# Delta rule: query norms as quadrant matmuls, alternating with the outputs' mean of squares in chunks of 256 columns

## What is computed

```python
q = heads(h @ Wq); k = heads(h @ Wk); v = heads(h @ Wv)
q = q / (norm(q) + 1e-6)
k = k / (norm(k) + 1e-6)
# for each token t, state s is 64x64 for each head and sequence
s = s * alpha[..., None]
pred = einsum('bhk,bhkv->bhv', k_t, s)
s = s + (beta * k_t)[..., None] * (v_t - pred)[:, :, None, :]
y_t = einsum('bhk,bhkv->bhv', q_t, s)
# then
y = y * rsqrt(mean(y * y, over a head) + EPS) * head_norm_w
```

## Time and profile before

| | |
|---|---|
| median of 3 runs | 2277.33 us (2270.29 to 2285.75) |
| the profiled execution | 2267.57 us, its span 2265.9 us |
| delta rule, 29 whole steps | 1063.5 to 1841.8 us of the span: 778.3 us, 26.8 us a step |
| busy over the span | PE 2017.6, PEld 1438.0, DVE 1503.7, ACT 1109.6, POOL 649.8 us |

### The profile page before, as it was taken

The page is one execution under the profiler, slowest core; times in us unless marked ns, Lnnn a source line. Parts: engine busy times, 40 slices in busy tenths (PEclk is TensorE's granted clock), DMA queues, the critical chain, the costliest instruction groups (busy, mean ns, idle before and its releaser), DMA issues. The chain is left out here.

```text
span 2265.9 us, 92374 instructions
## 1 busy us (share of the span) xinstructions
PE 2017.6 (89%) x41611; PEld 1438.0 (63%) x41611; DVE 1503.7 (66%) x3186; ACT 1109.6 (49%) x1913; POOL 649.8 (29%) x603
## 2 busy tenths in 40 slices
PE   4999997899877697979999999999999997988998
PEld 2666665566535484237888888888888873456446
DVE  7999984466567735766877777777787774344104
ACT  1344445366576765664555444454454543244334
POOL 5766661111130001213333333333333332001000
PEclk8999999899989999978999999999999998996998
DMA  3000000000000001000000000000000001002001
GB/s 95 3 3 3 3 3 2 6 3 3 2 4 11 1 2 32 0 0 4 5 4 4 4 4 4 4 4 4 4 5 4 4 5 52 0 1 75 0 0 38
DMA packets 34585, 23.28 MB, mean 10 GB/s; under 512 B 14857, under 2 KB 30161, under 8 KB 34194
## 3 DMA queue, kind: packets, MB, share of 16 engines
q1 hardware_dynamic: 34194, 17.38, 2.9%
HBM read 15.27 MB, written 2.10 MB: 8 GB/s over the span
## 5 line engine op out<-in xcount | busy, mean ns | idle before, releaser
L1747 PEld LDWEIGHTS psum<-dr_kq,dr_kSq 64*64 64x64 f32 x6144 | 199.4, 136 | 66.9 <-issue 56.9
L1747 PE MATMUL psum<-dr_kq,dr_kSq 64*64 64x64 f32 x6144 | 225.5, 222 | 8.2 <-DVE dr_G L2353 3.1
L2054 ACT ACTIVATE dr_Y<-psum 128x256 f32<-128x256 f32 x160 | 63.0, 394 | 313.1 <-PE psum L1753 312.1
L1747 PE MATMUL psum<-dr_GT,dr_Y 64*64 64x32 f32 x5120 | 186.7, 221 | 11.6 <-issue 11.0
L1753 PE MATMUL psum<-dr_G,dr_CT 64*64 64x32 f32 x5120 | 186.9, 223 | 0.2
L1747 PEld LDWEIGHTS psum<-dr_GT,dr_Y 64*64 64x64 f32 x5120 | 166.0, 135 | 15.7 <-issue 11.3
L1753 PEld LDWEIGHTS psum<-dr_G,dr_CT 64*64 64x64 f32 x5120 | 167.6, 136 | 0.8 <-issue 0.5
L2143 POOL TENSOR_TENSOR dr_kSq<-dr_kSq,dr_decay 128x256 f32<-128x256 f32 x128 | 99.0, 774 | 215.3 <-PE psum L1747 212.3
L2344 DVE COPY_PREDICATED dr_PT<-dr_level_masks,psum 128x256 f32<-128x256 uint32 x192 | 102.7, 535 | 83.0 <-PE psum L1747 80.4
L1753 PEld LDWEIGHTS psum<-dr_Y,dr_GT 64*64 64x64 f32 x4096 | 135.0, 136 | 33.7 <-issue 32.0
L1753 PE MATMUL psum<-dr_Y,dr_GT 64*64 64x32 f32 x4096 | 147.1, 220 | 7.1 <-issue 5.7
(11 more groups left out here) (385 smaller groups left out, 5541.8 us busy)
## 6 DMA issues: line engine op xcount, KB each, us to landing
topk_w<-in_L_ffn_w_dram SPq DMA_DIRECT2D x16, 256.0 KB, 5.9
attn_w_x_rows<-in_x_dram SPq DMA_DIRECT2D x4, 512.0 KB, 5.4
out_dram<-store_rows SPq DMA_DIRECT2D x4, 512.0 KB, 3.6
dout_w<-in_L_attn_Wff_dram SPq DMA_DIRECT2D x3, 256.0 KB, 3.0
attn_w_rows<-in_L_attn_Wq_dram SPq DMA_DIRECT2D x1, 256.0 KB, 5.4
attn_w_rows<-in_L_attn_Wk_dram SPq DMA_DIRECT2D x1, 256.0 KB, 4.8
attn_w_rows<-in_L_attn_Wv_dram SPq DMA_DIRECT2D x1, 256.0 KB, 4.2
attn_w_rows<-in_L_attn_Wo_dram SPq DMA_DIRECT2D x1, 256.0 KB, 3.8
```

The lines of the kernel that those rows point to most:

```text
L1747: last = nc.tensor.matmul(out(r), lhsT(r), rhs(r), start=True, stop=True)
L2054: act.activation(half_of(Y[l], l, 0), ZG[:, ZS].rearrange("p (m l) -> p m l", l=1 << l), ACT.Copy).then_inc(z_kept[l], 1)
```

## The change

The full-array matmul of the query norms leaves `norms`. The one of `head_norm` is split up. A new function `head_norms` stands where `head_norm` stood and issues both, in two chunks of 256 columns: for each chunk two `cross` matmuls of 64x64 for the queries into F1 and two `stay` matmuls of 64x64 for the outputs into E0. It waits for all that either needed.

As the query part crosses over, the squared queries must lie in the other half of the partitions. So `square` squares only the keys, and a new `square_queries` squares the queries in two instructions of 64 partitions each, reading one half and writing the other. In ACT's list `square_queries` follows `square_y`, `log_queries` moves behind `exp_norms`, and `query_eps` behind `inverse_y`. In `front` and `end`, which run once each, only one of the two sorts of matmul is issued.

```diff
@@ norms
             last.then_inc(n2_ready, 1)
-            nc.tensor.matmul(F1[:, :], w.head_sum[:, :], sq[:, 1, :], start=True, stop=True).then_inc(q2_ready, 1)
@@
-        def head_norm(w_, y):
-
-            u = par(w_)
+        def head_norms(w_, y):
+
             if y is not None:
                 pe.wait_ge(logn_ready, upto(y))
-            pe.wait_ge(floored, upto(w_))
-            nc.tensor.matmul(E0[:, :], w.head_mean[:, :], ysq[:, :], start=True, stop=True).then_inc(yms_ready, 1)
+                pe.wait_ge(q_squared, upto(y))
+            if w_ is not None:
+                pe.wait_ge(floored, upto(w_))
+            for at in (slice(0, 256), slice(256, 512)):
+                if y is not None:
+                    last_q = cross(lambda r: F1[r, at], lambda r: w.head_sum[r, r], lambda r: sq[r, 1, at])
+                if w_ is not None:
+                    last_m = stay(lambda r: E0[r, at], lambda r: w.head_mean[r, r], lambda r: ysq[r, at])
+            if y is not None:
+                last_q.then_inc(q2_ready, 1)
+            if w_ is not None:
+                last_m.then_inc(yms_ready, 1)
@@ PE, front
             values(y)
+            head_norms(None, y)
             diagonal(y)
@@ PE, end
-            head_norm(w_, None)
+            head_norms(w_, None)
@@ PE, half
-            if w_ is not None:
-                head_norm(w_, y)
+            if w_ is not None or y is not None:
+                head_norms(w_, y)
@@ ACT
-            act.activation(sq[:, :, :], kSq[par(y)][:, :, :], ACT.Square).then_inc(sq_ready, 1)
+            act.activation(sq[:, 0, :], kSq[par(y)][:, 0, :], ACT.Square).then_inc(sq_ready, 1)
+
+        def square_queries(y):
+
+            for j, r in enumerate(HALVES):
+                last = act.activation(sq[HALVES[1 - j], 1, :], kSq[par(y)][r, 1, :], ACT.Square)
+            last.then_inc(q_squared, 1)
@@ ACT, front
             square(y)
+            square_queries(y)
             exp_beta(y)
@@ ACT, half
                 square_y(w_)
             if y is not None:
+                square_queries(y)
                 log_norms(y)
-                log_queries(y)
                 exp_beta(y)
             keep_z(x, 3)
             if y is not None:
                 exp_norms(y)
-                query_eps(w_, y)
+                log_queries(y)
             if w_ is not None:
                 log_y(w_)
                 inverse_y(w_)
+            if y is not None:
+                query_eps(w_, y)
             keep_z(x, 4)
```

More of the change, by code:

```diff
@@ L1675, in delta_rule @@
     (zeroed, consts, h_staged, spikes_staged, logits, beta_ready, sig_ready, counted, pushed, raised, floored, paired, gates_ready, kq_logits, kSq_ready,
-     sq_ready, kq_ready, n2_ready, summed, counts_kept, biased, e_ready, logn_ready, norm_ready, length_ready, squared, denom_ready,
+     sq_ready, q_squared, kq_ready, n2_ready, summed, counts_kept, biased, e_ready, logn_ready, norm_ready, length_ready, squared, denom_ready,
      inverted, strong, turned, logq_ready, nq_ready, q2_ready, q_eps_ready, g0_made, gt0_made, v_ready, v_kept, diag_ready, diag_kept, rv_ready, rv_kept,
@@ L1680, in delta_rule @@
         "zeroed", "consts", "h_staged", "spikes_staged", "logits", "beta_ready", "sig_ready", "counted", "pushed", "raised", "floored", "paired", "gates_ready",
-        "kq_logits", "kSq_ready", "sq_ready", "kq_ready", "n2_ready", "summed", "counts_kept", "biased", "e_ready", "logn_ready",
+        "kq_logits", "kSq_ready", "sq_ready", "q_squared", "kq_ready", "n2_ready", "summed", "counts_kept", "biased", "e_ready", "logn_ready",
         "norm_ready", "length_ready", "squared", "denom_ready", "inverted", "strong", "turned", "logq_ready", "nq_ready", "q2_ready", "q_eps_ready", "g0_made",
```

## The result

| | before | after |
|---|---|---|
| median of 20 runs each | 2275.18 us (2262.32 to 2294.90) | 2263.89 us (2251.84 to 2276.59) |
| ratio | | 0.9954, 95% interval 0.9932 to 0.9976 |
| profiled execution, span | 2265.9 us | 2261.2 us |

The account below looks back on a forecast made before the run. PE was taken to set the pace, with DVE at 77% behind it. 33.6 us of PE work saved minus 1.9 us of waiting gave 31.7 us, from the median 2277.33 to 2245.6 us, 1.4% faster; range 2234 to 2271.

Parts of the forecast that it names:

- The array's work: PE in `norms` and `head_norms`: 1.06 us removed plus 0.06 us saved, 1.12 us a step, 33.6 us.
- Rivals B and C: `head_norms` quadrants: B two at a time, 2271 us, chance 0.09; C one at a time, 2322 us, chance 0.04.
- The rule of the Trainium skill on one PSUM bank and two row tiles: `head_norms`: different row tiles can't access one PSUM bank at once, so quadrants go two at a time; kept as a rival.
- DVE against POOL: `scale(x, 4)` on DVE loses 0.45 us behind POOL's `pair`; idle 0.46 us before `add_gt(x, 4)` covers it, costed at nothing.
- Rival A: After `pair`, POOL's `scale(x, 4)` goes first, DVE waits another 0.6 us, 18 us back, 2263.6 us; chance 0.16.
- `z_and_level(3)` waiting for `keep_ct(3)`: After `norms`, PE waits for DVE's `keep_ct(3)` in seven of 30 steps, about 1.9 us in all.
- The step that failed: PE sets the pace, its idle 1 to 2 us a step lying ahead of `norms`, waiting for ACT and DVE.
- The closing sentence: Wrong if PE's idle time ahead of `norms` grew by what it lost behind it; then DVE sets the step.

Follow-up runs that it names:

- the wide kernels: Kernels before and after the change with five parts each as one product of 512 columns, 280 records fewer a step; 0.9784 and 0.9705 of the kernel before.
- before_wide5: Kernel before the change with `level_zero`, `read_v`, `corrected`, `solve` and `outputs` each one product of 512 columns, 280 records fewer a step; ratio 0.9784.

## Why the prediction was wrong

**The array's work was right**, if by two errors that cancel. Forecast: `norms` 1.06 us shorter, the place of L1925 0.06. Measured: 0.94 and 0.19. `z_and_level(3)` starts 1.01 us after the first load of `norms` at the earliest and not 0.89. `head_norms` takes 0.70 us from its first weight load to the next part's in the step shown, not 1.00, but its last turn still runs then, and the first matmul of `g_and_gt(3)` starts 0.91 us after the first of `head_norms`. Sum 1.13 against 1.12. Rivals B and C are out: four turns, not eight or sixteen. The rule of the Trainium skill on one PSUM bank and two row tiles (TensorEngine Tiling (Array Packing), Restrictions and Gotchas) isn't borne out by the rows at 1201.02 to 1201.73 either, where each row group writes its own half of the bank's partitions.

**DVE against POOL was right in its cover.** The `scale` of decay on DVE went from 890 to 926 ns in the mean of 128, a seventh of a microsecond a step and not 0.45. The one of `scale(x, 4)` alone went from 0.96 to 1.13 us in the mean, where 1.45 was forecast. The wait of `add_gt` for PE fell from 14.6 us to 7.8, so the cover lasted. Rival A gave 2263.6 us, and 2263.9 was measured. That is chance: its mechanism, DVE giving the time back at `z_and_level(4)`, is not there. `diagonal, z_and_level(4)` takes 2.14 us in the mean, as before. A result that fits a rival's number isn't evidence for it.

**`z_and_level(3)` waiting for `keep_ct(3)` was right in kind**: by the times at which it ends, PE started late for it in 5 of 30 steps, 3.1 us in all where 1.9 was forecast. Of these, 2.1 us fall on the first step, where the kernel before lost 1.2 us in the same way. The view of waits, which covers the other 29, books 0.7.

**The step that failed** is the first one: that PE's idle time lies "ahead of `norms`, where PE waits for what ACT and DVE make", and that time taken from PE is taken from the path "as long as the other engines keep up". The other engines did keep up. PE's own instructions did not. The 1 to 2 us a step were mostly gaps on "issue" in the middle of parts, with no releaser, and I gave them to two engines that were already done. From that followed the missing term: 24 more records in a step and 1.1 us less to bring them in were costed at nothing. Measured, the time above the shortest parts rose by 0.77 us a step, 23 us:

- PE's gaps over 0.1 us: in the middle of a part 24.1 us in 41 gaps before, 30.4 in 55 after; at the start of a part 1.5 in 2 and 5.3 in 8. Together 10.1 us more in 20 more gaps. A gap costs somewhat more than this idle time, because the last matmul's record holds its way through the array. In the gap at 1413.69 it is some 0.2 us more, so I estimate 4 us more for 20 gaps.
- The clock. The granted clock was at its 1.2 GHz level for 6.8 us of the stage before and for 17.0 after, which costs half of that, 5 us. Four windows of the changed kernel show how that comes:

```profile
1482.00:1485.40 3.40, 2.85 (x124) 2.60 (x126) 1.14 (x4) 2.17 (x4) 0.64 (x1) 1.00 0.03 5
1485.40:1488.80 3.40, 2.28 (x91) 2.08 (x84) 2.91 (x6) 1.30 (x3) 0.00 (x0) 1.00 0.00 0
1488.80:1492.20 3.40, 3.40 (x75) 2.89 (x76) 0.79 (x2) 2.47 (x7) 2.89 (x3) 0.62 0.02 5
1492.20:1495.60 3.40, 3.40 (x108) 2.45 (x106) 2.85 (x16) 1.30 (x3) 1.39 (x2) 0.88 0.02 5
```

  PE is busy for 2.28 of 3.40 us, with one gap of 1.25 us on "issue" (by the weight loads), and right behind it the clock falls (0.62 in the mean of the window). Each of the six slow stretches of the two profiles begins 1.1 to 2.2 us after the end of a gap of 0.94 to 1.26 us by PE's records. But 16 of the 22 gaps of that length or more have no slow stretch behind them. That the gaps bring the slow stretches about is therefore likely and not shown.
- Some 4 us more are not told apart.

How the loss divides by cause: in the wide kernels some 0.4 of the 0.77 us come back, 0.10 are found at the wait for `keep_ct(3)`, another 0.1 or so in the gaps that are left there behind landed blocks, and 0.2 have no name. That is an account of the wide kernels, from one profile each. In the changed kernel itself the wait for `keep_ct(3)` costs 1.0 us in 29 steps, and 60 of 63 gaps end behind a block. By the device times alone, 18 us with about ±9 against 10.5, the 0.4 isn't certain. What makes the gaps is certain: before_wide5 took nearly all of them away with nothing but fewer instructions.

**The closing sentence** named what would make it wrong, PE's idle time growing ahead of `norms`, and drew the wrong conclusion from it (DVE). `outputs` did grow, by 0.18 us in the mean, through "issue".

## What to carry to other kernels

Before time taken from a busy engine is booked as gain, count its instructions for each microsecond and look at its gaps: "issue" in the middle of a run of like instructions was no other engine's doing here, and none of the reorderings tried mended it. Compare the shortest with the mean time of each part. What lies between is the time that a saving can vanish into. In such a stage instructions taken away can be worth more than columns saved (49 us for 280 of 1700 a step), and a change that trades columns for instructions may keep only part of its gain.

## What the runs showed of the hardware

- TensorE's instructions come in blocks of 16,384 bytes, 256 instructions. With 63 to 65 records a microsecond a block is needed every 4 us and gaps of 0.1 to 1.7 us open, of which 102 of 106 in two profiles end 1.2 to 1.65 us after a block has landed; with 56 they are all but gone. A block's own transfer took 0.9 to 1.5 us. Why the next records start only 1.2 us after the landing, no run shows.
- Four products of 64x64 and 256 columns in four quadrants run at once: 0.21 to 0.26 us a turn. Two of them write one bank from different row groups, each into its own half of the partitions.
- Waits that are met already are not free on PE: 64 of them, 32 instructions in the trace, cost 1.28 us a step.
